# A decoder layer with a mixture of experts: slot tables from one-hot products, and one sequence for all feed-forward tiles

## What is computed

```python
    probs = jax.nn.softmax(xn @ gate_w.T, axis=-1)
    tk_probs, tk_idx = jax.lax.top_k(probs, TOP_K)
    tk_probs = tk_probs / (jnp.sum(tk_probs, axis=-1, keepdims=True) + EPS)
    w = jnp.sum(tk_probs[..., None] * onehot, axis=1)      # onehot of tk_idx
    out = _swiglu(xf, sWg, sWu, sWd)                       # silu(x @ wg) * (x @ wu) @ wd
    for e in range(NUM_EXPERTS):
        out = out + w[:, e:e + 1] * _swiglu(xf, Wg[e], Wu[e], Wd[e])
```

## Time and profile before

| | us |
|---|---|
| median of 3 runs (lowest, highest) | 1984.34 (1980.09, 1992.53) |
| the profiled execution, its own time | 1987.56 |
| its span, first to last instruction | 1985.6 |
| TensorE busy in the span | 1786.8 |
| VectorE busy | 1252.0 |
| ScalarE busy | 1036.8 |
| feed-forward part, from its first transposes to the end | 1324.2 to 1985.6 |

### The profile page before, as it was taken

The page is one execution under the profiler, slowest core; times in us unless marked ns, Lnnn a source line. Parts: engine busy times, 40 slices in busy tenths (PEclk is TensorE's granted clock), DMA queues, the critical chain, the costliest instruction groups (busy, mean ns, idle before and its releaser), DMA issues. The chain is left out here.

```text
span 1985.6 us, 36115 instructions
## 1 busy us (share of the span) xinstructions
PE 1786.8 (90%) x11908; PEld 1179.4 (59%) x11909; DVE 1252.0 (63%) x2492; ACT 1036.8 (52%) x2238; POOL 407.6 (21%) x455
## 2 busy tenths in 40 slices
PE   6799999999999999889899999968419799999997
PEld 3343333333333333469779999957308688888886
DVE  6497999999999995241488999945206323223223
ACT  2205888788887888412378888842104233333332
POOL 3000000000000000220032222210660254554540
PEclk9856999999999999997999999988759899999998
DMA  5601121111211110242102010042003233333323
GB/s 173 179 7 26 29 45 30 27 27 34 43 28 26 27 28 3 72 147 101 68 28 70 18 68 17 24 154 95 14 13 106 63 48 53 52 49 53 51 50 122
DMA packets 90348, 112.51 MB, mean 57 GB/s; under 512 B 20156, under 2 KB 71792, under 8 KB 89168
## 3 DMA queue, kind: packets, MB, share of 16 engines
q1 hardware_dynamic: 73104, 91.27, 16.2%
q0 software_dynamic: 16032, 19.36, 6.0%
q10 hardware_dynamic: 1104, 0.43, 0.1%
HBM read 64.15 MB, written 38.48 MB: 52 GB/s over the span
## 5 line engine op out<-in xcount | busy, mean ns | idle before, releaser
L497 DVE TENSOR_REDUCE half_max<-psA 128x1 f32<-128x512 f32 x1024 | 634.6, 684 | 45.5 <-PE psA L547 45.1
L528 ACT ACTIVATE PT<-psB 128x1024 f32<-128x1024 f32 x512 | 517.5, 1025 | 173.7 <-PE psB L557 173.4
L547 PE MATMUL psA<-KS,QS 48*128 48x512 f32 x1024 | 410.4, 484 | 25.9 <-PEq L102 16.1
L557 PE MATMUL psB<-QS,KS 50*128 50x512 f32 x1024 | 367.3, 461 | 0.4 <-ACT PT L528 0.4
L576 PE MATMUL psO<-PT,VG 128*32 128x256 f32 x4096 | 332.4, 397 | 4.8 <-ACT OU L518 0.9
L547 PEld LDWEIGHTS psA<-KS,QS 48*128 48x128 f32 x1024 | 170.4, 197 | 252.9 <-DVE half_max L497 191.3
L576 PEld LDWEIGHTS psO<-PT,VG 128*32 128x32 f32 x4096 | 82.5, 108 | 192.8 <-issue 125.3
L2039 DVE TENSOR_TENSOR m_silu<-m_psU,m_silu 128x512 f32<-128x512 f32 x80 | 55.3, 692 | 200.9 <-PE m_psU L1997 200.9
L1348 ACT ACTIVATE x_probs<-x_scores,x_neg_max 128x77 f32<-128x77 f32 x512 | 176.3, 358 | 2.7 <-DVE x_neg_max L1254 2.6
L557 PEld LDWEIGHTS psB<-QS,KS 50*128 50x128 f32 x1024 | 146.6, 189 | 19.9 <-ACT PT L528 17.4
L1961 POOL DMA_INDIRECT acc<-m_y,tokens x72 | 114.6, 1592 | 169.4 <-DVE m_y L2055 169.4
(11 more groups left out here) (227 smaller groups left out, 2769.3 us busy)
## 6 DMA issues: line engine op xcount, KB each, us to landing
QS<-q_parts SPq DMA_DIRECT2D x96, 128.0 KB
q_parts<-part SPq DMA_DIRECT2D x16, 512.0 KB, 2.7
OT<-OU SPq DMA_DIRECT2D x32, 256.0 KB, 2.6
KS<-k_parts SPq DMA_DIRECT2D x32, 128.0 KB
xf_rows<-XF SPq DMA_DIRECT2D x32, 128.0 KB, 1.7
acc<-X SPq DMA_DIRECT2D x32, 128.0 KB, 1.8
WG<-in_Wg SPq DMA_DIRECT2D x8, 512.0 KB, 10.0
WU<-in_Wu SPq DMA_DIRECT2D x8, 512.0 KB, 10.5
```

Source lines behind the costliest of these rows:

```text
L497: dve.tensor_reduce(half_max[:, h * TB + t, n:n + 1], psA[:, bank_of(slot, 2 * v + r), :], axis=AX.X, op=ALU.max).then_inc(max_taken, 1)
L528: act.activation(PT[:, k % 4, 2 * a:2 * a + 2, :].rearrange("p h n -> p (h n)"), psB[:, u % 2, :, :].rearrange("p a n -> p (a n)"), ACT.Ex ...
L547: pe.matmul(psA[:, bank_of(slot, m), :], QS[top:top + KQ, slot, h // 2, t * P:(t + 1) * P], KS[top:top + KQ, slot, n * HALF:(n + 1) * HALF ...
L557: mm = pe.matmul(psB[:, u % 2, r, :], KS[top:top + KM, slot, c * P:(c + 1) * P], QS[top:top + KM, slot, a, half * HALF:(half + 1) * HALF], ...
```

## The change

The two phases become one, `phase_ffn`, with one sequence of 104 tiles: 24 shared, 72 of slots, 8 shared. The first 28 steps and the last 10 are straight code, and the loop between takes two steps per turn.

- Rows of the shared tiles are loaded from `xf_rows` in DRAM. The sum of a tile is loaded from `acc`, the output is added to it in one of three buffers, and stored again. `phase_cross` therefore stores X to `acc` for all 32 tiles, not for 8.
- SP's queue issues the two weight loads of one expert per step, in steps 0 to 7, behind the load of tile s+2.
- The routing operations are the same up to the slot, in larger pieces per step (`PIECES`).
- The scatter, its DRAM table and its read back are gone. In each of steps 7 to 14 VectorE makes one-hot rows for 8 columns of tokens (4 tiles x 2 choices): which row of a slot tile (128), and which slot tile (72), the latter times weight and times token number. In each of steps 8 to 15 TensorE multiplies them, 8 float32 products with 144 columns into one PSUM bank. The sum over all is token and weight of each slot. After step 16 VectorE writes `tokens` and `slots` from it.
- All eight experts' weights are split in steps 16 to 23, and the down weights loaded by SP there.
- The late tiles' loads of rows are issued up to four tiles ahead instead of three, so that one more stands before the 3 MB copy.

The diff, cut to its core:

```diff
@@ phase_cross @@
-                if i >= EARLY_TILES:
-                    sp.dma_start(T["acc"][i * P:(i + 1) * P, :], X[:, i, :]).then_inc(kept, 16)
+                sp.dma_start(T["acc"][i * P:(i + 1) * P, :], X[:, i, :]).then_inc(kept, 16)
@@ constants @@
-STRAIGHT = 14
-LOOPED = 6
-SPLIT_AT = {8: 6, 10: 7}
+COUNT_AT = 3
+HOT_AT = 7
+HOT = 4
+NHOT = NT // HOT
+COLS = HOT * TOP
+SPLIT_FROM = HOT_AT + NHOT + 1
+PIECES = [1, 1, 2, 1, 2, 2, 2, 1]
@@ steps @@
+            for s in range(EARLY_TILES + 4):
+                step(lambda lag, s=s: (s - lag, (s - lag) % 2) if s >= lag else None)
+                beside(s)
+            with eng.Fori(EARLY_TILES // 2 + 2, END // 2) as j:
+                for e in range(2):
+                    step(lambda lag, j=j, e=e: (j * 2 + (e - lag), (e - lag) % 2))
+            for s in range(END, NALL + 2):
+                step(lambda lag, s=s: (s - lag, (s - lag) % 2) if s - lag < NALL else None)
@@ SP @@
-            load(0, 0)
-            load(1, 1)
-            for n, x in enumerate(LOAD_ORDER):
-                for name in ("Wg", "Wu"):
-                    sp.dma_start(T[name.upper()][:, x, :, :], ...).then_inc(w_in[n // 2], 16)
+            load(0)
+            load(1)
+            for s in range(EARLY_TILES + 2):
+                if s + 2 < EARLY_TILES:
+                    load(s + 2)
+                if s < NE:
+                    for name in ("Wg", "Wu"):
+                        sp.dma_start(T[name.upper()][:, s, :, :], ...).then_inc(w_in, 16)
+                if 0 <= s - SPLIT_FROM < NE:
+                    if s == SPLIT_FROM:
+                        sp.wait_ge(slots_done, 5)
+                    sp.dma_start(WD[:, s - SPLIT_FROM, :, :], ...).then_inc(wd_in, 16)
+                if s >= 2:
+                    store(s - 2, acc)
+                if s < EARLY_TILES:
+                    load_sum(s)
+            for i in range(END, END + 4):
+                load(i)
+            sp.wait_ge(added, 16 * NTM)
+            load_sum(EARLY_TILES)
+            load_sum(EARLY_TILES + 1)
             sp.dma_start(out[0:first, :] ..., acc[0:first, :] ...).then_inc(copied, 16)
@@ POOL @@
-            pool.wait_ge(slots_in, 16)
-            pool.wait_ge(slots_done, 1)
-            for t in range(NT):
-                for c in range(TOP):
-                    pool.indirect_dma_start(out=slot_rows, out_offset=bass.IndirectOffsetOnAxis(ap=POS[:, c, t:t + 1], axis=0),
-                                            in_=own[:, c, t, :], in_offset=None).then_inc(scattered, 16)
-            pool.wait_ge(scattered, 16 * TOP * NT)
-            pool.dma_start(slots[:, :, :], rows).then_inc(slots_in, 16)
+            pool.wait_ge(slots_done, 5)
+            gather(EARLY_TILES)
@@ TensorE, beside the steps @@
+                q = s - HOT_AT - 1
+                if 0 <= q < NHOT:
+                    pe.wait_ge(hot_done, 4 * q + 4)
+                    for c in range(COLS):
+                        mm = pe.matmul(inverse, hot_row[:, q % 2, c, :], hot_tile[:, q % 2, c, :, :].rearrange("p v n -> p (v n)"),
+                                       start=(q == 0 and c == 0), stop=(q == NHOT - 1 and c == COLS - 1))
+                    mm.then_inc(inverted, 1)
@@ VectorE, one group of one-hot rows @@
+                dve.tensor_tensor(hot_tile[:, e, :, 0, :], numbers(tile_no, NTM), columns(slot_tile, NTM), ALU.is_equal).then_inc(hot_done, 1)
+                dve.tensor_tensor(hot_row[:, e, :, :], numbers(row_no, P), columns(slot_row, P), ALU.is_equal).then_inc(hot_done, 1)
+                dve.wait_ge(hot_done, 4 * q + 1)
+                dve.tensor_tensor(hot_tile[:, e, :, 1, :], hot_tile[:, e, :, 0, :], columns(weight, NTM), ALU.mult).then_inc(hot_done, 1)
+                dve.wait_ge(hot_done, 4 * q + 3)
+                dve.tensor_tensor(hot_tile[:, e, :, 0, :], hot_tile[:, e, :, 0, :], columns(token, NTM), ALU.mult).then_inc(hot_done, 1)
```

More of the change, by code:

```diff
@@ L1557, in phase_early, with phase_ffn @@
-def phase_early(nc, T):
-    X, XF, LG, tile_expert, slots, tokens = T["X"], T["XF"], T["LG"], T["tile_expert"], T["slots"], T["tokens"]
-    slot_rows, acc_t = T["slot_rows"], T["acc"].rearrange("(t p) d -> t p d", p=P)
-    t_done, y_in = T["tile_sems"][0], T["tile_sems"][-1]
+def phase_ffn(nc, T):
+    ident, LG, WD, tile_expert, slots, tokens = (T[k] for k in ("ident", "LG", "WD", "tile_expert", "slots", "tokens"))
+    xf_rows, acc = T["xf_rows"], T["acc"]
+    out = T["out"].rearrange("b s d -> (b s) d")
+    first = EARLY_TILES * P
+    SPLIT, SHARED = T["split"], T["shared_split"]
@@ new lines, in phase_ffn @@
+        counts_i = table("r_counts_i", [P, NE], I32)
+        tiles = table("r_tiles", [P, NE])
+        ends = table("r_ends", [P, 2, NE])
+        slot = table("r_slot", A3)
+        slot_of = table("r_slot_of", [P, NT, TOP])
+        slot_tile = table("r_slot_tile", [P, NT, TOP])
+        slot_row = table("r_slot_row", [P, NT, TOP])
+        slot_i = table("r_slot_i", [P, NT, TOP], I32)
+        weight = table("r_weight", [P, NT, TOP])
+        token = table("r_token", [P, NT, TOP])
+        tile_no = table("r_tile_no", [P, NTM])
@@ new lines, in phase_ffn, with shared, number, of_slots @@
+        NCONST = 7
+        block = ctx.enter_context(nc.Block())
+        def shared(i):
+            return isinstance(i, int) and (i < EARLY_TILES or i >= END)
+        def number(i):
+            return i if i < EARLY_TILES else i - NTM
+        def of_slots(i):
+            return i - EARLY_TILES
+        def steps(step, eng, beside=lambda s: None):
+            for s in range(EARLY_TILES + 4):
[6 more added lines that the diff above has]
+                step(lambda lag, s=s: (s - lag, (s - lag) % 2) if s - lag < NALL else None)
@@ new lines, in _ @@
+            for i in range(END, END + 4):
[3 more added lines that the diff above has]
+            load_sum(EARLY_TILES + 1)
+            sp.dma_start(out[0:first, :].rearrange("(p r) d -> p (r d)", p=P),
+                         acc[0:first, :].rearrange("(p r) d -> p (r d)", p=P)).then_inc(copied, 16)
+            for i in range(END, NALL):
+                if i + 4 < NALL:
+                    load(i + 4)
+                store(i, out)
+                if i + 2 < NALL:
+                    load_sum(number(i + 2))
@@ L2029, in step @@
             def step(tile):
-                if (t := tile(2)) and late(t[0]):
+                if (t := tile(2)) and shared(t[0]):
                     i, e = t
-                    dve.wait_ge(ht_high, base + i - NTM + 1)
+                    dve.wait_ge(ht_high, number(i) + 1)
                     dve.tensor_tensor(HL[1][:, e, :, :], psH[:, 0, :].rearrange("p (k n) -> p k n", n=P), HL[0][:, e, :, :],
```

716 lines of the change are left out of this document (272 added, 444 removed).

## The result

| | before | after |
|---|---|---|
| median of 4 runs (lowest, highest), us | 1985.07 (1980.09, 1992.53) | 1900.13 (1896.79, 1905.69) |
| the profiled execution, its own time | 1987.56 | 1896.79 |
| its span | 1985.6 | 1895.1 |
| feed-forward part, from its first transposes to the end | 661.4 | 575.2 |

The ratio is 0.9572 [0.9532, 0.9612]: faster, and 2 us above the predicted 1898. The spans differ by 90.5 us. Of these 86.2 lie in the feed-forward part, for which I had predicted 88. The other 4.3 us lie ahead of it (its first transposes start at 1319.90 instead of 1324.23), in phases that are the same but for the 24 added stores of X, which the prediction had costed at nothing. In the profiled executions of this study that start lies from 1315.7 to 1324.5 without these stores and from 1313.8 to 1323.6 with them.

The account below looks back on a forecast made before the run. TensorE bounds the slot-tile loop; the win lies in 168 us of stretches not full. 13.8 - 0.3 + 68.4 + 6 = 88 us off 1987.6 gives 1899.6, said as 1898; range 1884 to 1912 (0.70), to 1928 with rival A.

Parts of the forecast that it names:

- start, tile loads ahead of weights: Steps 0 to 3: TensorE's 12.62 us wait for tile 2 goes, 13.8 us won; first tile from DRAM loses 0.3.
- between, 211.2 us become: The 23 steps from step 3 to the first slot tile's step 26: 142.8 us instead of 211.2, 68.4 won.
- a step with products, from step 9: Eight float32 one-hot products on TensorE's path take 1.95 us, making the step 6.9 us.
- step 8: VectorE's expert numbers and first one-hot group stretch this step to 8.5 us (+3.6), with +2.0 for products on TensorE.
- wait in the tail: TensorE's 9.89 us wait behind the 3 MB copy shrinks to 5 us, now for the fifth late tile's load.
- tail, won: Late tiles: the fourth tile's load goes ahead of the 3 MB copy, 6 us won, between 4.9 and 7.
- rival A: One-hot products on TensorE slower than their columns say: at most 24 us more, 1922; chance 0.13.
- The stall: 1404 to 1488 us, 84 us: engines in straight code wait for instructions while the scatter occupies POOL's queue; goes with it.
- rival B: Fetch stall returns in longer straight code under gathers and adds: in full 69 us, 1967, chance 0.07; in part 0.06.
- What ends the phases' boundary: Before the first slot tile: 21.6 us go, since slots are known after step 16 and the first gather leaves at step 22.
- Rival D: Slots come too late and the first gather waits: a 40 us delay gives 1908, inside the range; no separate chance.
- C: Steps 0 to 8, SP's queue: weight loads starve the tiles, 101 + 39 us, 2038; chance 0.04, shared with other large losses.

Follow-up runs that it names:

- a_weightsfirst: Kernel after, with all 16 gate and up weight loads put ahead of tile 2's rows in SP's queue: 1913.61 us, ratio to before 0.9642.
- b_tilesfirst: Kernel before, with each step's tile load put ahead of its weight loads in SP's queue: 1973.9 us, ratio 0.9943.
- b_noscatter: Kernel before without the 64 indirect DMAs of the scatter, every slot naming the padding row: 1909.07 us, ratio 0.9631.
- b_latescatter: Kernel before, with all 64 indirect DMAs held back until the transposes of tile 16, when the loop runs: 1981.69 us.
- a_scatter: Kernel after, plus 64 indirect DMAs from POOL with rows of 8 bytes whose result nothing uses: 1955.41 us, ratio to before 0.9872.
- a_nohot: Kernel after without the one-hot rows and their products, every slot a padding row: 1874.4 us.
- a_wide: Kernel after, plus 64 unused indirect DMAs from POOL with rows of 512 bytes instead of 8: 1948.78 us.
- a_best: Kernel after, with the expert numbers worked out after step 15 and the 3 MB copy cut into 8 pieces: 1882.48 us, ratio to before 0.9483.

## Why the prediction held, and where its reasons did not

| step | predicted, us | measured |
|---|---|---|
| start, tile loads ahead of weights | 13.8 - 0.3 | 13.9 |
| between, 211.2 us become | 142.8 | 142.5 |
| a step with products, from step 9 | 6.9 | 6.83 |
| step 8 | 10.5 | 11.98 |
| a step with a split | 5.22 | 5.09 |
| wait in the tail | 5 | 5.02 |
| tail, won | 6 | 5.4 |
| 70 steps of slot tiles, lost | 0 | 1.8 |

*Start.* Right, from both sides by experiment. The first tile from DRAM costs nothing: TensorE waits 2.58 us for it, and 2.55 before. The 15.2 of a_weightsfirst all lie in step 2, in the wait of 14.02 and the slower clock behind it; the 12.0 of b_tilesfirst are 14.6 less the 2.4 that its later tiles wait. My 13.8 counted the slow step by an assumed share.

*Between.* The sum is right because its terms were taken from steps that stood alone in the trace, and partly by luck. Step 8 was 1.5 us too short. The time that VectorE keeps TensorE waiting was in the sum (3.6 us, and 3.33 were measured); the slower clock behind that wait, 1.6 us, was not. Steps 17 to 24, with the splits, gave 1.4 us back. The products cost what their columns say, 0.24 us each, so rival A did not come.

*The stall.* This is the step that failed, though its size was right. I wrote of "engines in straight code that wait for their next instructions while the scatter occupies POOL's queue". The number came from the trace (84 us nearly empty) and needed only that the stall goes with the scatter, which b_noscatter shows: 75.8 us, where rival B priced the stall at 69. The mechanism did not: b_latescatter has the same stall in a loop, and a_scatter has it with nothing waiting for the DMAs. What the runs showed in its place is that indirect DMAs in a dense train hold up engines whatever code they run; by what means stays open. Rival B rested on the failed reading. It asked whether the longer straight code would stall under gathers and adds; the question that decides is how densely the indirect DMAs follow each other. In the loop over slot tiles there are two per 5.1 us and POOL is busy half of the time, and TensorE is busy 370.00 of 370.00 us. The argument I gave against B, "two DMAs per step are not one each 1.27 us", was the true one, and deserved to be the whole of it. Another one misread the trace: the loop of before does not begin after the stall. Its first step is step 14, which TensorE opens at 1447.21, inside it. That the loop as such costs nothing is shown by b_noscatter, where the steps on both sides of its entry take 4.89 and 4.87 us.

The Trainium skill (SBUF — State Buffer, Who interferes with whom) says "DMA never contends with a compute engine" and knows only VectorE and POOL sharing a pair of ports. By that rule a train of DMAs from POOL would cost TensorE and ScalarE nothing. The runs differ: 62.1 us are lost in a_scatter, where no engine needs the data. The transfers need not be what contends; the signals and instructions of the engines come late.

*What ends the phases' boundary.* As predicted: the transposes of the first slot tile do not wait. The tokens are written at 1430.5, and the first gather goes out at 1460.0, when TensorE has freed its buffer; POOL's idle time of 140.6 us before it reaches back to its last operation at 1318.9. Rival D did not come, nor C: with a_weightsfirst one sees what starving would be, one wait of 14.02, and after has none.

*Tail and slot tiles.* The wait is as predicted and the tail won 5.4 us, but 1.8 us are lost in the loop over slot tiles, which I had at nothing: 70 of its steps take 361.7 us instead of 359.9. I found no wait that explains this; b_noscatter has the old length, so it belongs to the new code. It stays open.

*Accounts.* The stall 75.9 (steps 12 to 14 take 90.8 us before and 14.9 in b_noscatter), the start 13.9, the boundary 15.3 (20.2 us for the step before, 4.9 now) and the tail less the loss in the loop 3.6 make 108.7. Less 20.6 for the one-hot work that is 88.1, where 86.2 were measured. The last 1.9 us are in the rest of VectorE's work: steps 3 to 7, with the larger routing pieces, take 31.4 us instead of 25.9, and steps 8 to 24 take 85.5 in a_nohot instead of 89.1 in b_noscatter.

## What to carry to other kernels

When several engines wait at once for "issue" or "remote", look for a train of indirect DMAs beside them, and take it away, even if nobody needs its result. A wait every few DMAs also kept the stall away where it was tried (40 DMAs added to the kernel after); in the kernel before it was not tried. A table of 8192 entries is cheaper as 64 small products (20.6 us, on a full TensorE) than as 64 indirect DMAs (75.8 us of all engines). And in a queue shared by small loads that are due and large ones that are not, put the small ones ahead and cut the large ones: three places of this kernel gave 14, 5 and again 5 us.

## What the hardware showed that I had not expected

- Indirect DMAs from POOL, 1.27 us apart, bring the other engines nearly to a stop: PE busy 13.12 of 56 us. TensorE is held up from some 9 us after the first of them in the kernel before, 24 in a_scatter and 30 in a_wide, until 5 (a_scatter) to 12 us (before) after the start of the last. Why it comes earlier in the kernel before is open.
- In that state many instructions are issued 1.40 or 2.80 us apart, others (the output products of a_scatter from 1388.1) without a gap. Engines stand idle up to 43.7 us in one piece ("remote") for work that is done.
- The same bytes in plain DMAs from the same queue (0.54 us each) cost 1.5 us, and 40 indirect ones in groups of four 1.1 us.
- A wait of 3.33 us on TensorE in step 8 of after lets the output products and the eight float32 ones behind it take 5.06 us, at a granted clock of 0.67; behind the 0.95 of a_best they take 3.48, at 1.00. In the tail the waits of 5.02 (after) and 9.89 us (before) are each followed by 1.6 us of this kind in their own step and 0.7 and 1.1 in the next. So a wait costs 1.6 to 2.7 us again here, and not in proportion to its length.
